# Two transformer layers in one kernel: the first batch's queries and keys projected straight into the score strips, and the other projections moved to another step

## What is computed

```
layer 0: x = LN(x + attn0(x));  x = LN(x + ffn0(x))
layer 1: x = LN(x + attn1(x));  x = LN(x + ffn1(x))
attn0: 16 heads of 8 features, full softmax over 256 keys, qkv = x @ Wqkv + bqkv
ffn0:  128 -> 512, butterfly (9 stages), GELU, butterfly, 512 -> 128
attn1: low-rank q and kv, 4 key/value heads for 16 query heads, RoPE, causal softmax
ffn1:  gated (SiLU), int32 weights scaled by 1/127, 128 -> 384 -> 128
```

## Time and profile before

| | |
|---|---|
| median of 3 runs | 381.0 us (380.56 to 383.02) |
| the profiled execution | 382.55 us |
| its span, first to last instruction | 380.8 us |
| TensorE matmuls busy | 344.2 us (90%) |
| VectorE, ScalarE, GpSimd busy | 237.0 (62%), 204.2 (54%), 176.1 us (46%) |
| mean granted TensorE clock | 0.966 |

### The profile page before, as it was taken

The page is one execution under the profiler, slowest core; times in us unless marked ns, Lnnn a source line. Parts: engine busy times, 40 slices in busy tenths (PEclk is TensorE's granted clock), DMA queues, the critical chain, the costliest instruction groups (busy, mean ns, idle before and its releaser), DMA issues.

```text
span 380.8 us, 10496 instructions
## 1 busy us (share of the span) xinstructions
PE 344.2 (90%) x3912; PEld 240.1 (63%) x3912; DVE 237.0 (62%) x903; ACT 204.2 (54%) x439; POOL 176.1 (46%) x298
## 2 busy tenths in 40 slices
PE   3979999999989999899989799798999999999762
PEld 2556666565647556575559567496777778777551
DVE  3364657476748577475856567457688787853442
ACT  2014666665694656655593546725656565565310
POOL 7036963020202502355251965518957667374442
PEclk9996999999999999999998989879999999999988
DMA  4393150101010101101111102100112120000000
GB/s 152 54 292 58 34 135 5 30 3 30 3 29 2 31 3 31 30 2 30 30 31 29 28 4 53 30 8 15 30 32 55 33 51 12 18 16 1 17 14 14
DMA packets 9219, 14.04 MB, mean 37 GB/s; under 512 B 2001, under 2 KB 4945, under 8 KB 9041
## 3 DMA queue, kind: packets, MB, share of 16 engines
q1 hardware_dynamic: 8656, 13.11, 14.9%
q10 hardware_dynamic: 512, 0.26, 0.4%
HBM read 5.76 MB, written 1.05 MB: 18 GB/s over the span
## 4 chain that ended last, share of the span: by engine, by line
PE 78%; POOL 7%; DVE 5%; ACT 4%; issue 3%; DMA 2%; POOLq 0%; DVEq 0%; ACTq 0%
PE SM L283 27%; PE G L470 13%; PE ST L302 5%; PE G L367 5%; PE G L380 5%; PE G L356 4%; PE G L438 3%; PE G L339 3%; PE G L346 3%; PE G L389 2%; PE G L452 2%; POOL QK L787 2%; PE G L406 2%; DMA QK<-mt 2%; PE ST L444 1%
## 5 line engine op out<-in xcount | busy, mean ns | idle before, releaser
L526 ACT ACTIVATE E<-ST 128x512 f32<-128x512 f32 (+1 forms) x256 | 125.3, 541 | 89.3 <-PE ST L302 89.0
L302 PE MATMUL ST<-QK 32*128 32x256 f32 (+1 forms) x1024 | 138.8, 382 | 9.8 <-ACT E L526 8.0
L283 PE MATMUL SM<-QK 31*128 31x256 f32 (+1 forms) x1024 | 141.5, 382 | 0.6 <-DVE mx L652 0.5
L283 PEld LDWEIGHTS SM<-QK 31*128 31x128 f32 x1024 | 94.4, 188 | 40.4 <-DVE mx L652 13.3
L652 DVE TENSOR_REDUCE mx<-SM 128x2 f32<-128x512 f32 x128 | 82.3, 686 | 58.9 <-PE SM L283 58.8
L302 PEld LDWEIGHTS ST<-QK 32*128 32x128 f32 x1024 | 92.0, 188 | 14.0 <-ACT E L526 10.0
L660 DVE CUSTOM_DVE_ANT_0 masked_s<-SM,mask_sb 128x256 f32<-128x256 f32 (+1 forms) x256 | 75.7, 352 | 35.9 <-PE SM L283 35.7
L796 POOL TENSOR_SCALAR_AFFINE_SELECT E<-E 128x512 f32<-128x512 f32 x64 | 39.1, 635 | 40.5 <-ACT E L526 40.4
L470 PE MATMUL G<-E,V 128*32 128x256 f32 (+1 forms) x1024 | 55.1, 355 | 0.0
L470 PEld LDWEIGHTS G<-E,V 128*32 128x32 f32 x1024 | 29.3, 109 | 21.0 <-issue 5.0
L748 POOL TENSOR_SCALAR nm_a<-mv_a 128x2 f32<-128x2 f32 x16 | 3.1, 191 | 69.9 <-DVE mv_a L626 69.9
(11 more groups left out here) (107 smaller groups left out, 449.9 us busy)
## 6 DMA issues: line engine op xcount, KB each, us to landing
QK<-qk SPq DMA_DIRECT2D x62, 64.0 KB
rs<-ry SPq DMA_DIRECT2D x16, 128.0 KB, 2.3
xb<-x_nat SPq DMA_DIRECT2D x1, 1024.0 KB, 8.0
out<-ln_g SPq DMA_DIRECT2D x8, 128.0 KB, 2.0
xt<-x_t SPq DMA_DIRECT2D x1, 896.0 KB, 6.0
wi<-wi_all SPq DMA_DIRECT2D x1, 576.0 KB, 4.9
QK<-mt SPq DMA_DIRECT2D x32, 8.0 KB
fac<-fac_u SPq DMA_DIRECT2D x1, 508.0 KB, 4.6
```

The lines of the kernel that those rows point to most:

```text
L283: ins = nc.tensor.matmul(SM[m % S_RING][:, cols], q, QK[rows, b % QK_RING, r, 1, keys], start=True, stop=True)
L302: ins = nc.tensor.matmul(ST[m % S_RING][:, c * T:(c + 1) * T - q0], QK[rows, b % QK_RING, r, 1, c * P:(c + 1) * P], QK[rows, b % QK_RING, ...
L526: act.activation(E[:, a % E_RING, j, 0:n], ST[m % S_RING][:, 0:n], ACT.Exp, scale=SCALE)\
```

## The change

1. **First batch.** The weights for batch 0 come in a layout with zero columns (`wfirst`, four groups of 2 x 128 columns, and `bfirst`, whose value is 1.0 in row 31 of the keys), so that four projections (`first0` at FIRST, `first1` to `first3` at steps -14, -12 and -10) give the strips of batch 0 in place. ScalarE copies them with the bias into `QK[:, 0]`. The strips' DMAs, the DMA of ones and the zeroing of `QK[:, 0]` go for batch 0. Batches 1 and 2 are projected at steps -8 and 2 (`EARLY`), and ScalarE issues the four strip DMAs of batch 1.
2. **Warm-up.** VectorE sets a tile `idle` to zero before its other memsets; TensorE starts with three matmuls of 512 columns (six instructions) on it, where before it ran such matmuls on `QK` behind the projection of batch 0. Fillers start at step -8 and no longer at -14.
3. **SyncE's order.** The loads of the butterfly weights and others are issued in the beginning (`loads`); only x_nat and what follows it remains in the stepwise list, from step -2 on. `QK<-mt` stands ahead of the strip DMAs in a step.
4. **Projections.** `qk` moves from step 14 to step 6 of the period (`AT_QK` -34 to -42), `v` from step 0 to step 6, and both now stand ahead of `scores(g)` in TensorE's list. ScalarE's list keeps its order: the two exponentials of the step, then the copies of `qk` and V.
5. **Other places.** up0 from (50, 54, 56, 66) to (50, 56, 62, 66), dn0 from (70, 72) to (72, 78), the normalisation of the tile from 74 to 80, xt0 from 80 to 84, up1 from (34, 38, 40) to (34, 40, 44), RoPE from -28 to -34, its strips' DMAs from -24 to -28. The GELU stays at 66.
6. **O copies.** Those of the second half (t = 1) go from ScalarE to VectorE.

```
-AT_QK, AT_QKIN, AT_ROPE = -34, (-32, -24), -28
-AT_MT, AT_V, AT_PV = (-6, 2), 0, (12, 20)
+AT_QK, AT_QKIN, AT_ROPE = -42, -28, -34
+AT_MT, AT_V, AT_PV = (-6, 2), 6, (12, 20)
 AT_T, AT_ATT, AT_PROJ, AT_LN, AT_XT = 22, 24, 26, 28, 32
-AT_UP1, AT_DN1, AT_LN1 = (34, 38, 40), 46, 50
-AT_UP0, AT_GELU, AT_DN0, AT_LN0, AT_XT0 = (50, 54, 56, 66), 66, (70, 72), 74, 80
-BXU, BXD, TURN, JOIN, BV, XB_AT, WF_AT, LATE = (4, 6), 16, 32, 22, 0, 14, 38, -20
+AT_UP1, AT_DN1, AT_LN1 = (34, 40, 44), 46, 50
+AT_UP0, AT_GELU, AT_DN0, AT_LN0, AT_XT0 = (50, 56, 62, 66), 66, (72, 78), 80, 84
+BXU, BXD, TURN, JOIN, BV, XB_AT, WF_AT, LATE = (4, 6), 16, 32, 22, 0, 14, 38, -2
+FIRST_AT, EARLY, FILL = (FIRST, -14, -12, -10), (None, -8, 2), 8
+def projected_at(g):
+    if g in EARLY:
+        return EARLY.index(g)
+    b = batch_at(g, AT_QK)
+    return b if b is not None and b >= len(EARLY) else None
...
 SyncE:
+            sp.dma_start(wqk_sb[:, :, :], wqk0).then_inc(ld["qk"], 16)
+            sp.dma_start(bqk_sb[:, :], bqk0).then_inc(ld["qk"], 16)
...
+            for loaded, dst, src in loads:
+                sp.dma_start(dst, src).then_inc(loaded, 16)
...
 TensorE:
+            pe.wait_ge(idle_ready, 1)
+            for i in range(S_RING):
+                nc.tensor.matmul(ST[i][:, :], idle[:, 0:P], idle[:, :], start=True, stop=True)
             for g in STEPS:
+                if (b := projected_at(g)) is not None:
+                    x = xt[:, (b % NB) * T:(b % NB + 1) * T]
+                    if layer(b) == 0:
+                        bank = claim(("qk", b), A["qk_out"], 2 * b)
...
+                    else:
+                        bank = claim(("qk", b), A["y_out"], b - NB + 1)
...
+                if (b := batch_at(g, AT_V)) is not None:
+                    bank = claim(("v", b), A["v_ready"], b + 1)
...
                 scores(g)
+                for r in range(GROUPS):
+                    if g == FIRST_AT[r]:
+                        bank = claim(("first", r), first_out, 2 * (r + 1))
...
                 if (b := batch_at(g, AT_T)) is not None:
                     bank = claim(("t", b), A["at_ready"], b + 1)
-                    pe.wait_ge(A["o_ready"], 2 * (b + 1))
+                    for t in range(2):
+                        pe.wait_ge(A["o_ready"][t], b + 1)
...
-                if (b := batch_at(g, AT_QK)) is not None:
...
-                if g == FIRST:
-                    pe.wait_ge(zeros_ready, QK_RING)
...
-                if (b := batch_at(g, AT_V)) is not None:
...
 ScalarE:
-            act.dma_start(wqk_sb[:, :, :], wqk0).then_inc(ld["qk"], 16)
-            act.dma_start(bqk_sb[:, :], bqk0).then_inc(ld["qk"], 16)
-            act.dma_start(bv_sb[:, :], bv0).then_inc(ld["bvc"], 16)
+            act.dma_start(wfirst_sb[:, 0, :, :], wfirst[:, 0, :, :]).then_inc(ld["first"], 16)
+            act.dma_start(bfirst_sb[:, :, :], bfirst).then_inc(ld["first"], 16)
+            act.dma_start(wfirst_sb[:, 1:GROUPS, :, :], wfirst[:, 1:GROUPS, :, :]).then_inc(ld["groups"], 16)
...
-                            for j in range(2, STRIPS):
-                                act.dma_start(QK[STRIP * j:STRIP * j + ROWS, 0, :, :, :], qk[j:P:STRIPS, 0, :, :]).then_inc(qk_in[0], 16)
+                            for j in range(STRIPS):
+                                act.dma_start(QK[STRIP * j:STRIP * j + ROWS, 1, :, :, :], qk[j:P:STRIPS, 1, :, :]).then_inc(qk_in[1], 16)
...
 VectorE:
+            nc.vector.memset(idle[:, :], 0.0).then_inc(idle_ready, 1)
             nc.vector.memset(V[:, :, :, :], 0.0).then_inc(v_clean, 1)
...
+                if (b := batch_at(g, AT_PV[1])) is not None:
+                    dve.wait_ge(A["pv_ps"], 2 * (b + 1))
...
+                    nc.vector.tensor_copy(O[:, b % 2, 1, :], g_bank["pv", 2 * b + 1][:, 0:T]).then_inc(A["o_ready"][1], 1)
```

More of the change, by code:

```diff
@@ L88, in sem @@
             return ctx.enter_context(nc.semaphore(name))
+        wfirst_sb = sb("wfirst_sb", [P, GROUPS, 2, W])
+        bfirst_sb = sb("bfirst_sb", [P, GROUPS, 2])
+        idle = sb("idle", [P, 512])
         wqk_sb = sb("wqk_sb", [P, 2, W])
@@ L154, in block_kernel @@
         G = [ctx.enter_context(nc.psum_tensor(f"G{i}", [P, 512], F32)) for i in range(2)]
-        ld = {n: sem(f"ld_{n}") for n in ("x0", "x", "qk", "v", "id", "bf", "up", "bv", "bvc", "xb", "proj", "l1", "next", "rope", "gate")}
+        ld = {n: sem(f"ld_{n}") for n in ("x0", "x", "first", "groups", "qk", "v", "id", "bf", "up", "bv", "bvc", "xb", "proj", "l1", "next", "rope", "gate")}
         zeros_ready, v_clean, half_ready = sem("zeros_ready"), sem("v_clean"), sem("half_ready")
@@ L174, in block_kernel @@
             "up_ps", "th_ready", "hid_ready", "down_ps", "res_done", "var_ready", "ln_ready")}
+        A["o_ready"] = [sem(f"a_o_ready{t}") for t in range(2)]
         qk_in = [sem(f"qk_in{i}") for i in range(QK_RING)]
@@ L553, in _ @@
                     act.activation(xt[:, n * FT:(n + 1) * FT], g_bank["xt0", n][:, :], ACT.Copy).then_inc(F0["xt_ready"], 1)
[L554 to L555 removed]
+                for r in range(GROUPS):
+                    if g == FIRST_AT[r]:
+                        act.wait_ge(first_ps, r + 1)
+                        if r == 0:
+                            act.wait_ge(ld["first"], 32)
+                        for s in range(2):
+                            act.activation(QK[:, 0, r, s, :], g_bank["first", r][:, s * T:(s + 1) * T], ACT.Identity,
+                                           bias=bfirst_sb[:, r, s:s + 1]).then_inc(first_out, 1)
+                if (b := projected_at(g)) is not None:
+                    act.wait_ge(A["qk_ps"], b)
                     if layer(b) == 0:
[L557 to L559 removed]
+                        if b >= 3:
+                            act.wait_ge(qk_in[(b - 2) % QK_RING], 16 * STRIPS * loads_of(b - 2))
+                        elif b == 1:
                             act.wait_ge(ld["qk"], 32)
@@ L785, in _ @@
             nc.gpsimd.memset(half[:, :], -0.5).then_inc(half_ready, 1)
-            for i in range(QK_RING):
+            for i in range(1, QK_RING):
                 nc.gpsimd.memset(QK[:, i, :, :, :], 0.0).then_inc(zeros_ready, 1)
@@ L935, in _arrays @@
     kcol = [2 * D * (h // rep) + 2 * d, 2 * D * (vh // rep) + 2 * vd + 1]
+    wfirst, bfirst = np.zeros((P, GROUPS, 2, P), np.float32), np.zeros((P, GROUPS, 2), np.float32)
+    bfirst[MAXROW::STRIP, :, 1] = 1.0
+    for s, cols in enumerate((q, k)):
+        for i, c in enumerate(cols):
+            row, head = divmod(i, H)
+            to = STRIP * (head % STRIPS) + row
+            wfirst[:, head // STRIPS, s, to], bfirst[to, head // STRIPS, s] = wqkv[:, c], bqkv[c]
     u = np.concatenate([a["L0_ffn_W_exp"].T, a["L0_ffn_b_exp"][:, None]], 1)
```

164 lines of the change are left out of this document (84 added, 80 removed).

## The result

The median of 4 runs is 409.2 us (407.7 to 409.3, and one of 414.3 at a lower clock, which no comparison uses), against 381.0 (380.6 to 383.0) before; the ratio is 1.071, with a 95% interval of 1.065 to 1.076. The direction was forecast and the size was not: 391.5 was predicted, with a range up to 401, and the loss is 28 us instead of 10.5.

The account below looks back on a forecast made before the run. TensorE, busy over nine tenths of the span, was taken to bound the kernel. Gains and small terms of -20.7, +22.7 for the new wait and +8.5 for the clock gave +10.5: median 391.5 us, range 376 to 401.

Parts of the forecast that it names:

- the new wait: At transpose `T` (once `bxu1`), TensorE waits for ScalarE's projection copy queued behind two exponentials: +22.7 us, bounds 20 to 25.
- about half of them are followed by a fall: Behind ten new stops of 1.66 to 2.06 us, five clock falls at 1.7 each: +8.5 us, bounds 0 and 34.
- GELU: At the four GELU steps, `qk` and `v` fill 1.7 us of each TensorE stop: -6.5 us.
- Start: Before head 0: it comes at 25.6 instead of 28.55, -3.0 us, bounds -1 and -5.5.
- the sum from 2.0 to 9.4: Warm-up at the start: from 2.0, 3.9 us at half pace, then 3.5 at full pace, ending at 9.4.
- The credit for the clock's fall behind head 0: Clock fall at 30.3, which cost 3.4 us: half credited as its preceding wait becomes shorter, -1.7 us.
- This work is only moved: At the GELU steps, moving `qk` and `v` ahead of the stalling scores adds no work and fills 1.7 us per stop.
- does what it says and nothing else: Rival: no wait at all at `T`, giving -20.7 us and 360.3 us; chance 0.04.
- the clock's balance: Granted-clock terms: -1.7 behind head 0, -6.8 for layer 1's three falls, +8.5 for falls behind new stops.
- The normalised rows: -2: TensorE's 6.6 us of waits for normalised rows: the long stop goes, -2 us, bounds 0 and -4.
- ten short falls: Rival of more falls than half, behind the new stops: ten of the shorter kind cost 17 us, giving 400.
- the 20.7 us of gains: Sum of all terms except the new wait and the clock behind it: -20.7 us.

Follow-up runs that it names:

- the kernel with the copies first: The changed kernel with ScalarE's copy of the projection ahead of the two exponentials of its step: 378.9 us, ratio 0.989.
- one without stops: The changed kernel with the projection's copy ahead of the exponentials, RoPE at -30 and its strips' DMAs at -26: 372.7 us, ratio 0.978.
- the second kernel: The kernel before with only `qk` and `v` moved to step 6 ahead of the scores, and the `up1` places that needs: 426.6 us, ratio 1.118.

## Why the prediction was wrong

**Right: the new wait.** +22.7 was worked out and 21.7 measured, in 13 stops of 1.3 to 2.0, as many as forecast, and a small one of 0.3. The reading of the earlier trace rows (exponentials, copy, wake) held to 0.2 us for each, and the kernel with the copies first shows the cause. The forecast that about half of them are followed by a fall (five of ten long ones) held too: six of 13, counting the one that begins inside a stop.

**Right in the main: GELU** -6.5, measured -6.1. **Start:** -3.0, measured -4.7 at the scores of step 0 and -5.4 at head 0. What I had wrong is the pace of the warm-up. Its 5.47 us in the earlier trace rows were not at full clock, and I doubled a length that was already the slow one. The last of its six instructions, in the kernel before and in the kernel after:

```profile
12.33 1.04 PE L444 MATMUL ST<-QK 128*128 128x512 f32 x1
```

```profile
5.55 0.59 PE L364 MATMUL ST<-idle 128*128 128x512 f32 x1
```

Before, all six started 0.85 us or more apart, up to the next instruction at 13.18. After, they did so only up to 5.07; the last two took 0.48 and 0.43 to the next start. So the sum from 2.0 to 9.4 rests on a term, 3.9 us at half pace of 1.82 us for each, that no run shows: the six took 4.65 us. The credit for the clock's fall behind head 0 (half of 3.4) came in whole in the kernel after, where the stop for head 0 is down to 0.58 us; with only the start changed the stop is 1.64 us, and the fall is there.

**Wrong, and the largest: "This work is only moved".** The prediction said so of `qk` and `v` at the GELU steps, and at all other steps it let the move cost nothing but the wait. Moved work costs at its new place what it takes there (1.5 in a period of layer 0, measured) and gives back at its old place only what TensorE isn't held up for there anyway (0.26). I had not asked what the moved work itself had covered. The trace of before had a sign that there was something to cover. I had read the waits of TensorE's matmuls alone; those of its weight loads, in the kernel before, have this row:

```profile
PEld SM L283 <- DVE mx L652: 13.3, 29, 0.8
```

With 8.2 us in 22 for the maxima of layer 1, TensorE stood close against the maxima 51 times, with little of it seen in a matmul. It is a sign and not the price: the same waits are 21.7 us in 46 in the kernel after. The term left out is +10.9 in the kernel after and +14.5 in one without stops, where no stop can hide part of it; another 1.1 is batch 2's projection between these points. That the time is lost in the steps that the projections left is shown, by the five points and by the matmuls added there. What bounds these steps is shown in part, VectorE's rate for a quarter to a third; the rest stays open. The left-out term is also why "does what it says and nothing else" was put at 360.3 and the kernel without stops for a copy of `qk` or for `xt0` took 372.7.

**Wrong: the clock's balance.** -1.7 - 6.8 + 8.5 = 0 was the sum, +5.1 ahead of the tail (and -1.7 in it) is the measurement. All four falls of before did go or move, and seven came: five short and two long, one of them behind a stop that was not in the prediction. I priced all new falls at the shorter kind, and the earlier trace rows had half of them long. Six at the mean of before, 10.2 / 4 = 2.56, would have been 15.4 instead of 8.5; that seven cost just this is chance. Nor did each fall of before begin behind a stop: that of 245.34 begins inside the one that ends at 245.58. The Trainium skill (TensorE: Matmul & The Clock Gate, "Loop structure matters more than you think") says that a copy out of PSUM doesn't break the warm clock if matmuls follow at once. The runs agree, if its condition is read with it: with copies that TensorE stands for, so that the matmuls don't follow at once, the mean granted clock is 0.960, and with the same copies ahead of the exponentials, so that they do, 0.994. The prediction read it as setting this term to 0, and at these stops its condition isn't met.

**Missed: GpSimd's queue.** "The normalised rows: -2" came out at -1.9 by accident. The batch's waits of 6.6 went altogether and 4.7 for the tile's came, because RoPE and its normalisation changed places. The prediction had looked at RoPE's new place as more time for the strips, and named no queue that it passed. **The O copies** on VectorE were costed at nothing; with the projections moved they take away waits of 8.6 us of `v`, as the second kernel shows, so the sum was right to count little for `v` and didn't say to what it owed it. **Small ones:** `xt` -1.7 as forecast, `dn1` +1.5 where +1 was set down for `up1`, waits for maxima +1.3 that weren't in the sum.

In the profiled spans +25.1 was measured where +10.5 was forecast. Of the 14.6 between them, 10.9 is the left-out term, 1.1 batch 2's projection and 5.1 the clock; all others together are -2.5. The medians lie 3.1 further apart than the profiled executions, as the one of before was above its median and that of after below its own.

The range failed for the same reason. Its upper end of 401 was ten short falls; it had no case in which the 20.7 us of gains were smaller, though two of their terms were arguments and not rows.

## What to carry to other kernels

Moving work off a step shortens that step only if nothing else holds it up: read what the engine waits for there, its weight loads too, and credit only what is left when the wait is uncovered. Lost time of this kind may stand in no list of waits: compare the time between two like points of both traces, and the busy time in it. When lists are in order and a buffer is shared in turn, count which task last used the buffer and where its copy stands in the other engine's list; here one constant (`v` at 0 or 6) or the place of one copy decided over 27 to 30 us. And for every moved step, go through each engine's queue that it passes, as RoPE came to stand ahead of a normalisation here that TensorE was waiting for.

## What the runs showed of the hardware

Stops of TensorE of 1.3 to 2.0 us, a few each 100 us, cost more than their length: without the stops of `T` six of seven stretches at 1.2 GHz were gone, 27.3 us of them, and with `xt0`'s waits gone too none was left ahead of the tail (mean granted clock 0.960, 0.994, 0.997). Which of the stops is followed by a fall I can't say from the rows. Six of 13 were; the 3.29 us of `xt0` had a fall behind them in the kernel after and none with the copies first; and the 1.05 us for an exponential had one with the copies first and none with RoPE moved as well. TensorE's first matmuls run at the slower pace, on zeros too: 512 columns took 0.85 us from start to start up to 13.2 us in the kernel before and up to 5.1 us in the kernel after, then 0.43 (after). The profile's clock row says 1.00 there in both, so in the beginning the lengths have to be read and not the row. Four DMAs issued by ScalarE in a row kept it for 4.65 us, 1.16 each on average, while the same engine's three issues of weights at the very beginning took 0.41 to 0.45 each.
